# Attention block: six bf16 score products become three rounded-fp32 ones, with two heads on the two halves of the array's rows

## The reference

```python
qkv = jnp.einsum('bnd,ed->bne', inputs, w_in)
scores = jnp.einsum('bhqd,bhkd->bhqk', q, k) * Hd ** (-0.5)
scores = jnp.where(causal, -jnp.inf, scores)
attn = jax.nn.softmax(scores, axis=-1)
out = jnp.einsum('bhqk,bhkd->bhqd', attn, v)
```

## Time and profile before

| | |
|---|---|
| median of 3 runs | 1738.19 us (1734.22 to 1741.68) |
| the profiled execution | 1726.74 us, span 1725.1 us |
| mean granted TensorE clock | 0.947 |
| PE busy | 1449.8 us (84%) |
| PE weight loads busy | 755.3 us (44%) |
| DVE busy | 1180.8 us (68%) |
| ACT busy | 911.7 us (53%) |
| POOL busy | 734.0 us (43%) |
| DMA | 102.98 MB, mean 60 GB/s |

### The profile page before, as it was taken

How to read it: one execution, slowest core, us unless ns; L and a number is a source line. 1 busy time by engine, 2 the same in 40 slices (tenths; PEclk the granted TensorE clock), 3 DMA queues, 4 the chain that set the end, 5 groups by cost and what they waited for, 6 DMA issues and landing times.

```text
span 1725.1 us, 33029 instructions
## 1 busy us (share of the span) xinstructions
PE 1449.8 (84%) x10024; PEld 755.3 (44%) x10024; DVE 1180.8 (68%) x2306; ACT 911.7 (53%) x1795; POOL 734.0 (43%) x876
## 2 busy tenths in 40 slices
PE   3798998788998988989898888978889789889754
PEld 2353344344543444444453444434454344544343
DVE  4668676867677776777668675787757777677342
ACT  2056655655555555565545655555545655565612
POOL 2213314454353533555344543444445453344456
PEclk9789999999998999899998999999999999999968
DMA  3211122111311122111211113111122112211100
GB/s 104 55 63 49 48 78 74 57 39 56 100 64 35 52 69 88 56 53 51 96 51 49 46 57 101 55 38 50 57 91 69 41 44 68 70 57 49 50 33 25
DMA packets 101873, 102.98 MB, mean 60 GB/s; under 512 B 21296, under 2 KB 89912, under 8 KB 101696
## 3 DMA queue, kind: packets, MB, share of 16 engines
q1 hardware_dynamic: 98176, 91.59, 16.4%
q0 software_dynamic: 2560, 8.39, 1.3%
q10 hardware_dynamic: 960, 0.79, 0.2%
HBM read 31.74 MB, written 8.94 MB: 24 GB/s over the span
## 4 chain that ended last, share of the span: by engine, by line
PE 48%; DVE 21%; issue 12%; ACT 9%; POOL 5%; SPq 2%; DMA 2%; DVEq 1%; ACTq 0%; POOLq 0%
PE row_ps L1073 9%; PE val_ps L1097 9%; PE col_ps L1043 8%; PE dense_ps L1107 7%; DVE max_a L868 7%; PE dense_ps L1109 5%; PE dense_ps L1108 5%; ACT weights L712 4%; DVE mixed L981 3%; PE row_ps L1078 2%; DVE max_b L868 2%; PE dense_ps L1126 2%; DVE xn_c L907 1%; SPq L458 1%; DVE gated L965 1%
## 5 line engine op out<-in xcount | busy, mean ns | idle before, releaser
L712 ACT ACTIVATE weights<-col_ps 128x512 f32<-128x512 f32 (+1 forms) x1216 | 620.9, 580 | 473.0 <-PE col_ps L1043 470.9
L868 DVE TENSOR_REDUCE max_a<-row_ps 128x1 f32<-128x512 f32 (+3 forms) x864 | 550.3, 663 | 238.3 <-PE row_ps L1078 155.3
L1073 PE MATMUL row_ps<-k_stack,q_stack 96*128 96x512 bf16 (+3 forms) x1536 | 469.8, 344 | 51.6 <-DVE max_a L868 33.3
L1043 PE MATMUL col_ps<-q_stack,k_stack 99*128 99x512 bf16 (+3 forms) x1536 | 400.8, 337 | 54.0 <-ACT weights L712 33.8
L594 POOL TENSOR_SCALAR_AFFINE_SELECT weights<-weights 128x512 f32<-128x512 f32 x256 | 171.0, 668 | 543.2 <-ACT weights L712 541.1
L1097 PE MATMUL val_ps<-weights,v_ones 128*32 128x512 f32 (+3 forms) x3072 | 337.0, 511 | 16.7 <-POOL weights L594 16.1
L1073 PEld LDWEIGHTS row_ps<-k_stack,q_stack 96*128 96x128 bf16 x1536 | 146.7, 100 | 354.4 <-DVE max_a L868 168.1
L868 DVE TENSOR_REDUCE max_b<-row_ps 128x1 f32<-128x384 f32 (+3 forms) x352 | 213.2, 635 | 115.0 <-PE row_ps L1078 114.7
L1043 PEld LDWEIGHTS col_ps<-q_stack,k_stack 99*128 99x128 bf16 x1536 | 133.5, 99 | 221.3 <-ACT weights L712 138.3
L1078 PE MATMUL row_ps<-causal,ident_bf 128*128 128x128 bf16 x1024 | 207.4, 227 | 0.0
L1078 PEld LDWEIGHTS row_ps<-causal,ident_bf 128*128 128x128 bf16 x1024 | 104.4, 102 | 14.8 <-issue 0.5
(11 more groups left out here) (127 smaller groups left out, 2251.6 us busy)
## 6 DMA issues: line engine op xcount, KB each, us to landing
q_stack<-q_part SPq DMA_DIRECT2D x384, 64.0 KB, 2.5
k_stack<-k_part SPq DMA_DIRECT2D x372, 64.0 KB, 2.5
xa<-in_x SPq DMA_DIRECT2D x8, 1024.0 KB, 6.6
att<-val_out SPq DMA_DIRECT2D x64, 128.0 KB
recips<-recip_rows SPq DMA_DIRECT2D x32, 256.0 KB
xq<-in_x SPq DMA_DIRECT2D x28, 256.0 KB, 3.0
out<-xq POOLq DMA_DIRECT2D x28, 256.0 KB, 2.6
q_stack<-max_rows SPq DMA_DIRECT2D x192, 4.0 KB
```

The costliest lines, as they stand in the source:

```text
L712: nc.scalar.activation(weights[:, t % 2, h:h + n, 0:q1 - q0], col_ps[bank][:, 0:n * (q1 - q0)].rearrange("p (h q) -> p h q", h=n), ACT.Exp ...
L868: nc.vector.reduce_max(dest, bank[:, 0:len(heads) * (k1 - k0)].rearrange("p (h k) -> p h k", h=len(heads)), AX_X).then_inc(max_done, 1)
L1043: last = nc.tensor.matmul(col_ps[bank][:, i * (q1 - q0):(i + 1) * (q1 - q0)], k_stack[s % 2][:, h, P * j:P * (j + 1)], q_stack[s % 2][:, h ...
L1073: last = nc.tensor.matmul(bank[:, n * width:(n + 1) * width], q_stack[stack][0:ROWS, h, P * i:P * (i + 1)], k_stack[stack][0:ROWS, h, k0:k ...
```

## The change

q, k and the maxima are held as two rounded fp32 parts instead of three bf16 parts, with three products of parts instead of six: 3 x 16 = 48 rows, and 50 with the two rows of maxima. Heads 0 and 2 of a group lie on rows 0 to 63 of the stacks, heads 1 and 3 on rows 64 to 127. Each score matmul of an even head is followed by that of an odd head on the other half of the rows, into another bank. The mask of a diagonal block is added by two matmuls of 64 rows (128 and 64 columns) per head. A bank holds at most two heads, so a unit of 128 columns has two units of 256 instead of one of 512: 40 row units and 40 column units per quarter instead of 38. All row pairs of a step are issued between its column pairs, before values and dense products. POOL no longer splits q and k; the maxima are transposed by one fp32 transpose instead of four bf16 ones; SP places them with four DMAs instead of three. Stack DMAs keep their number and bytes (six per side and half of the tokens, each now from 32 partitions in runs of 2 KB where it was 64 partitions in runs of 1 KB). `recept` and `k_relu` share the buffers of `mix_out` and `h2_diff`. The weights' columns are reordered on the host. The diff, cut to what matters:

```diff
-Q_PARTS = (0, 0, 0, 1, 1, 2)
-K_PARTS = (0, 1, 2, 0, 1, 0)
+Q_PARTS = (0, 0, 1)
+K_PARTS = (0, 1, 0)
 ROWS = len(Q_PARTS) * HD
-MROWS = 3
-FILL = 2 * len(Q_PARTS) * 16
+MROWS = 2
+ROW_TILE = 64
+FILL = 2 * 2 * len(Q_PARTS) * 16
+PLACED = 2 * MROWS * 16
...
+def bank_heads(width):
+    return ((0, 2), (1, 3)) if width <= QT else ((0,), (1,), (2,), (3,))
...
-PER_STEP = [2, 3, 3, 3, 3, 4, 4, 5, 5, 4, 2, 1]
+PER_STEP = [2, 4, 2, 4, 5, 4, 4, 4, 4, 4, 2, 2]
...
-        q_stack = [sb(f"q_stack{i}", [ROWS + MROWS, G, N], BF16) for i in range(2)]
+        q_stack = [sb(f"q_stack{i}", [P, 2, G // 2, HALF], F32R) for i in range(2)]
...
-        recept = sb("recept", [P, 2, D])
-        k_relu = sb("k_relu", [P, KC, QT])
+        recept = mix_out
+        k_relu = h2_diff
...
-                hold(parts_done, b * 8 + (8 * (s // 4) + 4 * (s % 4 // 2) + 2 * (half + 1)))
+                hold(free["qk"], b * 8 + (8 * (s // 4) + 4 * (s % 4 // 2) + 2 * (half + 1)))
...
-                        sp.dma_start(stack[buf][HD * r:HD * (r + 1), :, cols],
-                                     parts[part][lo:lo + 64, cols]).then_inc(stack_filled[buf][half], 16)
+                        for odd in range(2):
+                            at, lo = ROW_TILE * odd + HD * r, 64 * (s % 2) + 32 * odd
+                            sp.dma_start(stack[buf][at:at + HD, half].bitcast(F32),
+                                         parts[part][lo:lo + 32, cols].bitcast(F32)
+                                         ).then_inc(stack_filled[buf][half], 16)
+
+            def place_max(stack, half):
+
+                for part in range(MROWS):
+                    for odd in range(2):
+                        row, lo = ROW_TILE * odd + ROWS + part, 8 * (2 * part + odd)
+                        sp.dma_start(stack[row:row + 1, half].rearrange("p g n -> p (g n)").bitcast(F32),
+                                     max_rows[half][lo:lo + 8, :].bitcast(F32)).then_inc(max_placed[half], 16)
...
-                    wait_apart(pool, "pool", free["qk"], count)
-                    nc.gpsimd.tensor_copy(side[1][:, cols], qk_rest[:]).then_inc(part2_done, 1)
-                    pool.wait_ge(part2_done, count)
-                    nc.gpsimd.tensor_tensor(side[2][:, cols], qk_rest[:], side[1][:, cols],
-                                            ALU.subtract).then_inc(parts_done, 1)
...
-                    wait(act, free["value"], q)
+                    wait(act, out_done, q)
                     nc.scalar.activation(recept[:], dense_ps[:], ACT.Tanh, scale=0.5).then_inc(free["recept"], 1)
...
-                    nc.vector.tensor_copy(max_rows[half][:], bank[:].bitcast(BF16)[0:3 * G, 0:HALF]
-                                          ).then_inc(max_done, 1)
+                    nc.vector.tensor_copy(max_rows[half][:], bank[0:2 * MROWS * 8, 0:P]).then_inc(max_done, 1)
...
-                nc.vector.scalar_tensor_tensor(max_rest[:], src, -1.0, parts[:, :, 0:G], ALU.mult,
-                                               ALU.subtract).then_inc(max_chain, 1)
-                dve.wait_ge(max_chain, chain + 2)
-                nc.vector.tensor_copy(parts[:, :, G:2 * G], max_rest[:]).then_inc(max_chain, 1)
-                dve.wait_ge(max_chain, chain + 3)
-                nc.vector.tensor_tensor(parts[:, :, 2 * G:3 * G], max_rest[:], parts[:, :, G:2 * G],
-                                        ALU.subtract).then_inc(max_split, 1)
+                nc.vector.scalar_tensor_tensor(lo, src, -1.0, hi.bitcast(F32), ALU.mult,
+                                               ALU.subtract).then_inc(max_split, 1)
...
-                    wait(dve, parts_done, count - 1)
-                    nc.vector.tensor_tensor(qk_rest[:], dense_flat,
-                                            side[0][:, HALF * half:HALF * (half + 1)],
+                    nc.vector.tensor_tensor(side[1][:, cols], dense_flat, side[0][:, cols].bitcast(F32),
                                             ALU.subtract).then_inc(free["qk"], 1)
...
+                pair = COL_HEADS[t][c - COL_FIRST[t]:c - COL_FIRST[t] + 2]
+                for i in range(len(pair[0])):
+                    for odd, heads in enumerate(pair):
+                        bank, ago = bank_of(COLS * s + c + odd, COLS * G)
+                        if i == 0:
+                            wait(pe, exp_done, exp_index(b, s, c + odd) + (1 - ago))
+                        rows = slice(ROW_TILE * odd, ROW_TILE * odd + ROWS + MROWS)
+                        last = nc.tensor.matmul(col_ps[bank][:, i * (q1 - q0):(i + 1) * (q1 - q0)],
+                                                stack_at(k_stack[s % 2], rows, heads[i], P * j, P * (j + 1)),
+                                                stack_at(q_stack[s % 2], rows, heads[i], q0, q1),
+                                                start=(i == 0), stop=(i == len(heads) - 1), skip_group_check=True)
+                        if i == len(heads) - 1:
+                            last.then_inc(cols_ready, 1)
...
+                for n in range(len(pair[0])) if diagonal else ():
+                    for a in range(2):
+                        for odd in range(2):
+                            rows = slice(ROW_TILE * odd, ROW_TILE * (odd + 1))
+                            end = n == len(pair[0]) - 1 and a == 1
+                            last = nc.tensor.matmul(banks[odd][:, (n + 1) * width - P + ROW_TILE * a:(n + 1) * width],
+                                                    mask_ident[rows, a, :], mask_fill[rows, a, ROW_TILE * a:P],
+                                                    start=False, stop=end, skip_group_check=True)
...
-                    work = (4 * cols + 4 * has_values + 6 * bool(unit) + 6 * len(backs_now)) or 1
+                    work = 4 if cols else (4 * has_values + 6 * bool(unit) + 6 * len(backs_now)) or 1
```

More of the change, by code:

```diff
@@ L66, in row_units @@
         for second, (k0, k1) in enumerate(spans):
-            width = k1 - k0
-            heads = min(G, HALF // width)
-            heads = 1 if heads == 3 else heads
-            units += [(i, range(h, h + heads), k0, k1, second) for h in range(0, G, heads)]
+            units += [(i, heads, k0, k1, second) for heads in bank_heads(k1 - k0)]
     return units
@@ L817, in _ @@
             for i in range(2):
-                nc.vector.memset(k_stack[i][ROWS:ROWS + MROWS, :, :], 1.0)
+                for odd in range(2):
+                    rows = slice(ROW_TILE * odd + 32, ROW_TILE * (odd + 1))
+                    nc.vector.memset(k_stack[i][rows].bitcast(F32), 1.0)
+                nc.vector.memset(max_parts[i][:].bitcast(F32), 0.0)
             dve.wait_ge(w_hi_done, 1)
@@ L1028, in _, with stack_at @@
             last.then_inc(mod_ready, 1)
-            pe.wait_ge(consts_done, 1)
+            pe.wait_ge(consts_done, 3)
             pe.wait_ge(setup_done, 3)
+            def stack_at(stack, rows, head, n0, n1):
+                half = n0 // HALF
+                return stack[rows, half, head // 2, n0 - HALF * half:n1 - HALF * half]
             def score_columns(b, s, t, c):
                 q0, q1, j = COL_STEPS[t]
-                n = COL_HEADS[t]
                 if c in (0, COL_FIRST[4]):
-                    pe.wait_ge(max_placed[t // 4], b * (48 * G) + 48 * (s + 1))
-                bank, ago = bank_of(COLS * s + c, COLS * G)
-                wait(pe, exp_done, exp_index(b, s, c) + (1 - ago))
-                for i in range(n):
-                    h = (c - COL_FIRST[t]) * n + i
-                    last = nc.tensor.matmul(col_ps[bank][:, i * (q1 - q0):(i + 1) * (q1 - q0)],
-                                            k_stack[s % 2][:, h, P * j:P * (j + 1)],
-                                            q_stack[s % 2][:, h, q0:q1], start=(i == 0), stop=(i == n - 1),
-                                            skip_group_check=True)
-                last.then_inc(cols_ready, 1)
@@ L1070, in row_unit @@
                 diagonal = k1 == P * (i + 1)
-                for n, h in enumerate(heads):
-                    end = n == len(heads) - 1
-                    last = nc.tensor.matmul(bank[:, n * width:(n + 1) * width],
-                                            q_stack[stack][0:ROWS, h, P * i:P * (i + 1)],
-                                            k_stack[stack][0:ROWS, h, k0:k1],
-                                            start=(n == 0), stop=(end and not diagonal), skip_group_check=True)
-                    if diagonal:
-                        last = nc.tensor.matmul(bank[:, (n + 1) * width - P:(n + 1) * width], ident_bf[:],
-                                                causal[:], start=False, stop=end, skip_group_check=True)
@@ L1080, in row_unit @@
-                last.then_inc(rows_ready, 1)
+                banks = [None, None]
+                for n in range(len(pair[0])):
+                    for odd, heads in enumerate(pair):
+                        if n == 0:
+                            banks[odd] = row_bank(b, s, u + odd)
```

(11 more changed lines are left out.)

133 lines of the change are left out of this document (68 added, 65 removed).

## The result

The changed kernel took 1999.35 us (median of 4 runs, 1975.70 to 2008.03), the kernel before 1737.72 beside it: a ratio of 1.146 [1.135, 1.157], 15% slower. Forecast were 1655 us and "faster". The ratio leaves out the slowest of the four runs (2008.03 us, over 1.5% above the fastest), so it isn't the quotient of the two medians.

A forecast was written before the change was run, and what follows sets the result against it. PE was taken as the bound, shared with DVE in s = 1. Saving 10.0 us per batch over 7.6 batches and 4 at the start, 1726.7 became 1647, written as 1655 us; 8-in-10 range 1560 to 1745.

The forecast's parts named there:

- The sum: Whole run: 76 us saved in the middle and 4 at the start, from 1726.7 to 1647 us, written as 1655.
- The clock eats it: Rival, all quarters: emptier quarters fall to clock 0.87, about +13 us per batch, 1757 us, counted as no change; chance 0.07.
- Issue order: Row pairs ahead of values and dense products in each step: costed at nothing; 14 us per batch if DVE's cover fails.
- Streams in pairs: PE's scores: a pair costs one stream, 0.22 us at 512 columns, 8.6 us per quarter instead of 16.2.
- the second always waits for its bank: Score part of each step: one way for pairs not to overlap, PE's list growing 3.6 us per quarter.
- the pairs run one after another: Rival, score part of each step: no overlap of row halves, +7.5 us per batch, 1795 us; chance 0.15.
- weight loads in series: Rival, paired scores: loads don't overlap, each fp32 matmul costs 0.11 us, -3.9 us per batch, 1708 us; chance 0.13.
- Changes of shape: PE between scores, values and dense products: 0.09 us each, one more per dense unit, 0.8 us per quarter.
- DVE and POOL: Vector work: DVE saves 2.4 us per batch; POOL's savings bring nothing in the middle, 4 us at the start.
- PE busy about 155 us: Sign of a right forecast: PE's busy time in windows of a middle batch, after 23.2 us saved per batch.
- SP's queue at step 4: Key DMAs behind maxima DMAs in s = 1 to 3: 4.0 us per batch of gain lost, 1.9 added.
- How the gain was converted: Per batch: 297.2 us of PE and DVE work at 1.605 busy engines gives 185.1 us, 15.9 less.

The follow-up runs named there:

- 6: Kernel before with its scores on 66 rows, without nearly all of the last two partial products and without the maxima: 1855.3 us, 1.065.
- 5: Kernel before with scores and masks on 64 rows, two of six products, the maxima and half of each mask left out: 1883.4, 1938.5 and 1964.1 us.
- 12: Kernel before with its stacks filled to 128 rows by zeros in q against ones in k, scores unchanged: 1723.7 us, 0.994.
- 10: Changed kernel with both heads of a pair, and the masks, on rows 0 to 63, so nothing can overlap: 2326.1 us, 1.335.
- 13: Changed kernel with each half filled to 64 rows (62 for row scores) by zeros in q against ones in k: 1950.3 us, 1.123.
- 9: Changed kernel with the old proportion of row scores among the other work, first pair still beside the columns: 1917.6 us, 1.110.
- 11: Changed kernel with scores and masks on all 128 rows, no overlap, and the old proportion of row scores among other work: 1838.1 us, 1.057.
- 7: Changed kernel with scores and masks on all 128 rows, maxima to a spare buffer, two heads mixed per product: 1888.1 us, 1.090.
- 14: Changed kernel with each half filled to 64 rows and the old proportion of row scores among other work: 1845.4 us, 1.064.
- number 4: Kernel before with only the new order of issue, row scores of a step beside its column scores: 1844.4 us, 1.068.
- number 3: Kernel before with its scores, not masks, on 64 rows, unpaired, two of six products and the maxima left out: 2133.1 us, 1.235.

## Why the prediction was wrong

**The sum has no term for the clock: this is the step that failed.** All its prices are for the upper level, in a kernel that was to keep its 0.947. "The clock eats it" (0.07) was the right rival, sized far too small and tied to the wrong thing: it let every quarter fall to 0.87, the lowest of the earlier trace rows, for want of work, and came to 1757 us. The clock was 0.784 over the run, 0.71 in s = 1, and 0.80 in s = 0, where PE is busy for 60 of 68 us. What lowers it here isn't waits alone but how many of the array's rows the work loads, and the pairs halve the time for which scores load it. Shown by 6 (66 rows, 0.857), 5 (64 rows, 0.832), 12 (125 to 128 rows, up by 0.02), 10 (about 50 rows, 0.713 at 91% busy) and 13 (up by 0.03 from rows of zeros times ones).

**"Issue order: I cost it at nothing" was wrong too**, as "the weakest term" might be: +6.8% on the kernel before, 3.2%, 3.1% and 5.2% given back in the three pairs of runs with the old proportion (9, 11 against 7, 14 against 13). The text's own price for the failure, 14 us per batch or 106 us in all, is within 8 us of number 4's 114 (1844.4 less 1730.2), but that is luck, since it isn't the way described: DVE's idle time ahead of the two groups of maxima didn't grow (number 4). It is PE that waits. A row score that has no bank holds up the values and dense products queued behind it; the text looked for the harm on the engine that empties the banks and not on the one that fills them.

**Streams in pairs: the mechanism right, its price not.** The sum took every pair as one stream, 0.22 us at 512 columns. In the changed kernel's trace that holds neither for all pairs nor in full: 573 of 1536 don't start together, most of them for want of a bank, and those of 512 columns that do start together, at the upper level, have the next matmul behind them after a median of 0.24 us (a column pair after a row pair), 0.29 (masks) or 0.34 (a row pair after a column pair); at 128 columns it is 0.11 to 0.16 for the 0.12 of the sum. What the extra is isn't shown. So "the second always waits for its bank", named under "the pairs run one after another" (0.15), came true for about a quarter of the pairs (399); that this rival's 1795 us lies nearest to the outcome is luck all the same, as it has no clock in it. Of "weight loads in series" (0.13) the sign, 0.11 us per matmul at every width, was not seen. The rule of the Trainium skill (TensorE: Matmul & The Clock Gate, Part 3) that tiles of different rows run concurrently agrees with the pairs that start together, 3 ns apart in the median.

**Changes of shape: right in size.** 0.09 was taken, 0.10 measured (number 3, in both directions). The drain of which the Trainium skill (TensorEngine Tiling (Array Packing), Key Properties) warns costs that here.

**DVE and POOL: right in sign.** DVE's busy time over the run fell from 1180.8 to 1106.7 us, 9.3 per batch where 2.4 was worked out. 64 more maxima were to cost 0.36 us per quarter, 11.5 in all, but the two groups of maxima together went from 763.5 to 756.2 us. A cast in the splitting of the maxima (11.6 us) goes too, which the term left out. And work that the change doesn't touch got cheaper: `mixed` from 76.2 to 63.4 us, `xn_c` from 33.8 to 21.2; why, no run shows. POOL's went from 734.0 to 614.1.

**"PE busy about 155 us": wrong**, 207.9. Busy time times the clock of its quarter, a rough measure, is 169 us per batch before and 165 after: even at an even clock only 4 of the expected 23 us showed as busy time. The late second matmuls of the pairs, and pairs dearer than one stream, are the part of this that the trace names.

**"SP's queue at step 4": not reached.** `DMA k_stack` releases the row scores for 21.6 us in all (loads and matmuls together), where the kernel before has 31.0; the steps before it grew longer instead of shorter, so this bound had no occasion. It is neither confirmed nor refuted.

**How the gain was converted** (PE and DVE at 1.605 engines) rested on an unchanged clock and went down with it. In the changed kernel the same sum is (207.9 + 136.0) / 240.3 = 1.431.

**Slips in the working**, none of which decides: 96 matmuls at 0.11 us are 10.6, not 11.0; the 1708 and 1795 us of two rivals leave out the 4 us of the start; and the 20 to 23 us of the clock rival are counted from a clock of 1.00, where the earlier trace rows already has 0.96 (from there it is 16).

What stays open: the 5 to 6% that 11 and 14 still lack. Number 11 has the clock of the kernel before, so its 5.7% is something else: PE is busy for 1591.9 us for 1449.8, and without overlap the prediction itself had 21.7 us of scores, masks and changes per quarter for 18.1. Number 14 has the lower clock and the late second matmuls. How much of each is due to these, to the first pair that still stands beside the columns, to the two split units per quarter and to the fourth DMA of maxima was not taken apart. Nor was it tried whether rows filled with other values than zero would lift the clock more.

## What to carry to other kernels

Packing two small matmuls on PE's rows halves the time for which they load the array; where the granted clock is already below 1.00 in some stage, price the step as "the rest of PE's work at a lower clock" before counting the gain, and try first what costs nothing: filling unused rows with zeros times ones. A change that takes several operations ahead of others "beside" a third needs the number of buffers between them checked: with three banks and two taken at once, the third waits, and everything queued behind it on that engine too. Before counting on an overlap, ask also whether the second of the pair will have its buffer when the first starts.

## What was not expected of the hardware

- With the same instructions, order and widths, 66 rows for 96 to 99 in the scores took the granted clock from 0.92 to 0.95 down to 0.84 to 0.86 and cost 6.5%.
- In number 10 the clock fell after 10 us with PE busy for 9.55 and stayed at 1.2 GHz for 58 us with PE busy for 57.85; over that whole run, with PE busy for 91%, it was 0.713.
- Rows that multiply zeros by ones count: 28 of them per pair moved the clock from 0.784 to 0.817, 29 in the kernel before from about 0.934 to 0.953 (means of 13 and 10 runs).
- A matmul on 64 rows next to one on 128 costs 0.10 us of PE's time each way; one on 66 rows next to 128 costs nothing that the timeline shows.
- Two score matmuls on the two halves of the rows start some 3 ns apart when both banks are free, and take 0.24 to 0.34 us at 512 columns where one stream is 0.22.
- Executions of one kernel can differ: number 5 took 1883 to 1964 us, with clocks of 0.832 to 0.792, while number 10, at 0.712 to 0.717, stayed within 2318 and 2328. The cause isn't known.
